# The expert stage's front with its router as the stationary operand and its rows normalised by ScalarE

## The reference, cut to what matters

```python
def _L1_ffn_ref(x, gate_w, gate_b, sw1, sb1, sw2, sb2, rw1, rb1, rw2, rb2):
    ...
    probs = jax.nn.softmax(x @ gate_w + gate_b, axis=-1)      # gate_w is 256 x 8
    topk_probs, topk_idx = jax.lax.top_k(probs, TOP_K)        # 2 of 8 experts
    cw = jnp.sum(jax.nn.one_hot(topk_idx, N_EXPERTS, dtype=x.dtype) * topk_probs[..., None], axis=2)
    hr = jnp.einsum('bsd,edf->ebsf', x, rw1) + rb1[:, None, None, :]
    out_e = jnp.einsum('ebsf,efd->ebsd', _swiglu(hr), rw2) + rb2[:, None, None, :]
    routed_out = jnp.einsum('ebsd,bse->bsd', out_e, cw)
    return shared_out + routed_out
...
x = x + 0.5 * _L0_ffn_ref(_layernorm(x, axis=-1), ...)
x = x + _L0_attn_ref(_layernorm(x, axis=-1), ...)
x = x + 0.5 * _L0_ffn_ref(_layernorm(x, axis=-1), ...)
x = x + 0.5 * _L1_ffn_ref(_layernorm(x, axis=-1), ...)
x = x + _L1_attn_ref(_layernorm(x, axis=-1), ...)
x = x + 0.5 * _L1_ffn_ref(_layernorm(x, axis=-1), ...)
```

## Time and profile before

| | us |
|---|---|
| three runs | 2554.85, 2563.77, 2571.64 |
| their median | 2563.77 |
| the profiled execution, its own time | 2565.47 |
| its span in the trace | 2563.6 |
| front of the first expert stage, first statistics to first use of the logits | 823.86 to 880.12 |
| the same of the second | 2088.27 to 2144.52 |

### The profile page before, as it was taken

One profiled execution on the slowest core, in us unless ns is written; L12 is line 12 of the kernel. 1 busy time (PEld: TensorE's weight loads), 2 busy tenths in 40 slices (PEclk: granted clock), 3 DMA queues, 4 the chain that ended last, 5 costly groups with the idle time before them and its releaser, 6 DMA issues. The chain is left out here.

```text
span 2563.6 us, 42162 instructions
## 1 busy us (share of the span) xinstructions
PE 2058.2 (80%) x11491; PEld 1356.1 (53%) x11492; DVE 1844.1 (72%) x3714; ACT 895.0 (35%) x1746; POOL 890.0 (35%) x889
## 2 busy tenths in 40 slices
PE   2599997689998658888776698998989865788885
PEld 1366666556665646677555233333333454567764
DVE  5698874498886776668976676776767377666696
ACT  1222224322222323333255255554555422233331
POOL 1344432144443656665245000000000035666641
PEclk9799997899999569999989699988989885899997
DMA  4000001100001512223336443334242024122234
GB/s 161 1 1 0 0 0 26 25 1 1 0 0 42 171 58 80 80 78 108 106 81 145 69 63 45 54 57 62 37 57 31 1 79 153 58 81 79 81 119 141
DMA packets 110245, 155.69 MB, mean 61 GB/s; under 512 B 20758, under 2 KB 77372, under 8 KB 109628
## 3 DMA queue, kind: packets, MB, share of 16 engines
q1 hardware_dynamic: 90416, 104.43, 18.1%
q0 software_dynamic: 17472, 48.80, 5.9%
q10 hardware_dynamic: 2252, 1.29, 0.2%
HBM read 107.00 MB, written 47.20 MB: 60 GB/s over the span
## 5 line engine op out<-in xcount | busy, mean ns | idle before, releaser
L1882 DVE TENSOR_REDUCE t_nm<-ps 128x1 f32<-128x512 f32 (+3 forms) x768 | 391.1, 552 | 152.9 <-PE ps L1972 75.4
L1948 ACT ACTIVATE t_E<-ps 128x1024 f32<-128x1024 f32 (+3 forms) x384 | 295.6, 808 | 280.1 <-PE ps L1998 225.9
L1377 PE MATMUL ps<-m_w,m_xT 128*128 (+1 forms) x1248 | 348.4, 415 | 0.0
L1377 PEld LDWEIGHTS ps<-m_w,m_xT 128*128 128x128 f32 x1248 | 223.5, 190 | 54.7 <-issue 4.4
L535 PE MATMUL ps<-wgT,f_xT 128*128 128x352 f32 x512 | 188.2, 517 | 37.0 <-DVE f_h L437 35.0
L496 POOL TENSOR_TENSOR f_h<-f_h,f_hmagic 128x704 f32<-128x704 f32 x64 | 108.0, 1688 | 298.4 <-DVE f_h L182 298.4
L1995 PE MATMUL ps<-t_Qs,t_Ks 98*128 98x512 bf16 (+3 forms) x768 | 208.0, 352 | 4.4 <-DMA t_Qs<-t_mT 3.4
L1867 POOL COPY t_Va<-t_V 128x128 f32 (+1 forms) x64 | 16.1, 295 | 542.2 <-DVE t_mp L1893 541.7
L1397 PE MATMUL ps<-m_w,m_hT 128*128 (+1 forms) x1248 | 202.0, 298 | 0.7 <-DVE m_hT L1476 0.7
L569 PE MATMUL ps<-wdT,f_hT 128*128 128x256 f32 (+1 forms) x768 | 191.1, 391 | 7.4 <-DVE X L472 5.4
L1967 PE MATMUL ps<-t_Ks,t_Qs 48*128 48x512 bf16 (+3 forms) x384 | 137.9, 359 | 70.4 <-DVE t_nm L1882 47.0
(11 more groups left out here) (285 smaller groups left out, 4078.0 us busy)
## 6 DMA issues: line engine op xcount, KB each, us to landing
m_yl<-m_picked_out SPq DMA_DIRECT2D x64, 256.0 KB, 2.8
m_raw<-in_L_ffn_rw SPq DMA_DIRECT2D x48, 256.0 KB, 3.3
t_parts<-t_qkv_part SPq DMA_DIRECT2D x64, 192.0 KB, 2.8
t_Qs<-t_parts SPq DMA_DIRECT2D x96, 128.0 KB, 4.2
t_Ks<-t_parts SPq DMA_DIRECT2D x96, 128.0 KB, 6.9
m_rows<-m_xn SPq DMA_DIRECT2D x16, 512.0 KB, 4.1
m_xg<-m_rows POOLq DMA_DIRECT2D x64, 128.0 KB, 3.1
X<-in_L_attn_x SPq DMA_DIRECT2D x4, 1024.0 KB, 14.2
```

What stands on the lines that cost most here:

```text
L1377: last = nc.tensor.matmul(ps[:, H1 + u, :], xT[:, u, kx, k, :], of_expert(w1, kw, e, k), start=n == 0, stop=n == 3 * DC - 1)
L1882: nc.vector.tensor_reduce(dst, ps[:, bank, 0:n], AX_X, ALU.max, negate=True).then_inc(emptied, 1)
L1948: nc.scalar.activation(E[:, s % NPB, :, 0:n], ps[:, bank:bank + 2, 0:n], ACT.Exp, scale=float(HD) ** -0.5).then_inc(e_ok, 1)
```

## The change

Three things change in the front, and their waits with them.

1. The logits: the router (16 or 8 columns) becomes the stationary operand and the 512 tokens of a group move, 4 matmuls in a group. The result has 16 rows by 512 tokens, in PSUM bank 6 or 7; ScalarE copies it to SBUF (`rows_from`), and TensorE turns it back with 4 transposes (`turn_logits`) into bank 4, as before.
2. `x_normalise` moves from VectorE to ScalarE, as scale times x plus a shift; the shift is made by a further VectorE and a further GpSimd instruction.
3. ScalarE's loop is written anew: `x_hi(g)`, `rows_from(g - 1)`, `x_normalise(g + 2)`, then the high halves of pieces 2g and 2g + 1, which stood at its head before.

```diff
--- before.py
+++ after.py
@@ -883,6 +883,7 @@
         w2 = ch.sb(name + "w2", [P, 2, SLOTS, FK, D], F32R, ctx=ctx)
         with ExitStack() as wctx:
             raw = ch.sb(name + "raw", [P, RAW, 512], ctx=wctx)
+            rowed = ch.sb(name + "rowed", [2 * EXPERTS, 2, GN], ctx=wctx)
         b1 = ch.sb(name + "b1", [P, SLOTS, 2 * FFE], ctx=ctx)
         b2 = ch.sb(name + "b2", [P, SLOTS, D], ctx=ctx)
         topw = ch.sb(name + "topw", [P, 2, TILES], ctx=ctx)
@@ -896,6 +897,8 @@
             router = ch.sb(name + "router", [P, DC, 2, EXPERTS], F32R, ctx=actx)
             mv = ch.sb(name + "mv", [P, 2, GT, 2], ctx=actx)
             veps = ch.sb(name + "veps", [P, 2, GT], ctx=actx)
+            nmean = ch.sb(name + "nmean", [P, 2, GT], ctx=actx)
+            shift = ch.sb(name + "shift", [P, 2, GT], ctx=actx)
             rstd = ch.sb(name + "rstd", [P, 2, GT], ctx=actx)
             small = ch.sb(name + "small", [P, 7, TILES], ctx=actx)
             taken = ch.sb(name + "taken", [P, TILES + 1, EXPERTS], BF16, ctx=actx)
@@ -918,7 +921,8 @@
                 sem, ("taken", "counted", "placed", "hot", "row_marked", "pick_marked", "tabled"))
             raw_in = [sem(f"raw_in{k}") for k in range(RAW)]
             xn_out = [sem(f"xn_out{k}") for k in range(2)]
-            XB_, LOGITS, COUNT, TABLE = (0, 1, 2, 3), 4, 5, 6
+            rows_ok, rows_out = sem("logit_rows"), sem("logit_rows_out")
+            LOGITS, COUNT, TABLE, ROWED = 4, 5, 6, (6, 7)
 
             def part(k):
 
@@ -954,6 +958,7 @@
                     for k in range(RAW + 2 * GROUPS, PIECES):
                         load_piece(k)
                     sp.wait_ge(w_split, PIECES)
+                    sp.wait_ge(logit_ok, GROUPS)
                     sp.dma_start(b1[:, 0:EXPERTS, :].rearrange("p e f -> p (e f)"),
                                  a['L1_ffn_rb1'].rearrange("e f -> (e f)").partition_broadcast(P)).then_inc(loaded_b, 16)
                     sp.dma_start(b1[:, SHARED, :], a['L1_ffn_sb1'][0].partition_broadcast(P)).then_inc(loaded_b, 16)
@@ -979,18 +984,10 @@
                         for j in range(GT):
                             nc.vector.bn_aggr(mv[:, b, j, :], ch.st6[:, j, :])
                         drain()
-                        ts(veps[:, b, :], mv[:, b, :, 1], EPS, None, ALU.add).then_inc(stats, 1)
-
-                    def x_normalise(g):
-                        b = g % 2
-                        dve.wait_ge(rstd_ok, g + 1)
                         if g >= 2:
-                            dve.wait_ge(x_turned, g - 1)
-                            dve.wait_ge(xn_out[b], 16 * (g // 2))
-                        for j in range(GT):
-                            last = ts(xn[:, b, j, :], ch.tile(g * GT + j), mv[:, b, j, 0:1], rstd[:, b, j:j + 1],
-                                      ALU.subtract, ALU.mult)
-                        last.then_inc(xn_ok, 1)
+                            dve.wait_ge(rstd_ok, g - 1)
+                        ts(veps[:, b, :], mv[:, b, :, 1], EPS, None, ALU.add)
+                        ts(nmean[:, b, :], mv[:, b, :, 0], -1.0, None, ALU.mult).then_inc(stats, 1)
 
                     def x_low(g):
                         dve.wait_ge(x_high, g + 1)
@@ -1017,10 +1014,7 @@
                     nc.vector.memset(taken[:, TILES, :], 0.0)
                     x_stats(0)
                     x_stats(1)
-                    x_normalise(0)
                     for g in range(GROUPS):
-                        if g + 1 < GROUPS:
-                            x_normalise(g + 1)
                         if g + 2 < GROUPS:
                             x_stats(g + 2)
                         x_low(g)
@@ -1140,8 +1134,12 @@
 
                     def x_rstd(g):
                         pool.wait_ge(stats, g + 1)
-                        nc.gpsimd.tensor_tensor(rstd[:, g % 2, :], veps[:, g % 2, :], ch.minus_half[:, :],
-                                                ALU.pow).then_inc(rstd_ok, 1)
+                        if g >= 2:
+                            pool.wait_ge(xn_ok, g - 1)
+                        nc.gpsimd.tensor_tensor(rstd[:, g % 2, :], veps[:, g % 2, :], ch.minus_half[:, :], ALU.pow)
+                        nc.gpsimd.drain()
+                        nc.gpsimd.tensor_tensor(shift[:, g % 2, :], nmean[:, g % 2, :], rstd[:, g % 2, :], ALU.mult
+                                                ).then_inc(rstd_ok, 1)
 
                     x_rstd(0)
                     x_rstd(1)
@@ -1178,15 +1176,24 @@
                         pe.wait_ge(x_stored, g + 1)
                         if g == 0:
                             pe.wait_ge(router_ok, 1)
+                        if g >= 2:
+                            pe.wait_ge(rows_out, g - 1)
+                        o = ps[0:2 * EXPERTS, ROWED[g % 2], :]
+                        for c in range(DC):
+                            nc.tensor.matmul(o, router[:, c, :, :].rearrange("p k e -> p (k e)"),
+                                             xT[:, g % 2, 0, c, :], start=c == 0, stop=False)
+                        for c in range(DC):
+                            last = nc.tensor.matmul(o[0:EXPERTS, :], router[:, c, 0, :],
+                                                    xT[:, g % 2, 1, c, :], start=False, stop=c == DC - 1)
+                        last.then_inc(rows_ok, 1)
+
+                    def turn_logits(g):
+                        pe.wait_ge(rows_out, g + 1)
                         for j in range(GT):
-                            o = ps[:, LOGITS, (g * GT + j) * 2 * EXPERTS:(g * GT + j + 1) * 2 * EXPERTS]
-                            for c in range(DC):
-                                nc.tensor.matmul(o, xT[:, g % 2, 0, c, j * P:(j + 1) * P],
-                                                 router[:, c, :, :].rearrange("p k e -> p (k e)"),
-                                                 start=c == 0, stop=False)
-                            for c in range(DC):
-                                last = nc.tensor.matmul(o[:, 0:EXPERTS], xT[:, g % 2, 1, c, j * P:(j + 1) * P],
-                                                        router[:, c, 0, :], start=False, stop=c == DC - 1)
+                            n = g * GT + j
+                            last = nc.tensor.transpose(ps[:, LOGITS, n * 2 * EXPERTS:(n + 1) * 2 * EXPERTS],
+                                                       rowed[:, g % 2, j * P:(j + 1) * P],
+                                                       ch.ident[0:2 * EXPERTS, 0:2 * EXPERTS])
                         last.then_inc(logit_ok, 1)
 
                     x_turn(0)
@@ -1194,6 +1201,9 @@
                         if g + 1 < GROUPS:
                             x_turn(g + 1)
                         logits(g)
+                        if g >= 1:
+                            turn_logits(g - 1)
+                    turn_logits(GROUPS - 1)
                     pe.wait_ge(taken_ok, 1)
                     every = (TILES + 1) * EXPERTS
                     nc.tensor.matmul(ps[:, COUNT, 0:every], ch.all_ones[:, :],
@@ -1226,15 +1236,40 @@
                     def x_hi(g):
                         act.wait_ge(x_turned, g + 1)
                         if g >= 2:
-                            act.wait_ge(logit_ok, g - 1)
+                            act.wait_ge(rows_ok, g - 1)
                         for c in range(DC):
                             last = nc.scalar.activation(xT[:, g % 2, 0, c, :], ps[:, 2 * (g % 2) + c, :], ACT.Copy)
                         last.then_inc(x_high, 1)
 
+                    def x_normalise(g):
+                        b = g % 2
+                        act.wait_ge(rstd_ok, g + 1)
+                        if g >= 2:
+                            act.wait_ge(x_turned, g - 1)
+                            act.wait_ge(xn_out[b], 16 * (g // 2))
+                        for j in range(GT):
+                            last = nc.scalar.activation(xn[:, b, j, :], ch.tile(g * GT + j), ACT.Identity,
+                                                        bias=shift[:, b, j:j + 1], scale=rstd[:, b, j:j + 1])
+                        last.then_inc(xn_ok, 1)
+
+                    def rows_from(g):
+                        act.wait_ge(rows_ok, g + 1)
+                        if g >= 2:
+                            act.wait_ge(logit_ok, g - 1)
+                        nc.scalar.activation(rowed[:, g % 2, :], ps[0:2 * EXPERTS, ROWED[g % 2], :], ACT.Copy
+                                             ).then_inc(rows_out, 1)
+
+                    x_normalise(0)
+                    x_normalise(1)
                     for g in range(GROUPS):
+                        x_hi(g)
+                        if g >= 1:
+                            rows_from(g - 1)
+                        if g + 2 < GROUPS:
+                            x_normalise(g + 2)
                         for k in range(2 * g, 2 * g + 2):
                             high_piece(k)
-                        x_hi(g)
+                    rows_from(GROUPS - 1)
```

## The result

The changed kernel takes 2591.89 us (median of 4 runs, 2584.92 to 2601.71), the kernel before 2560.64 (4 runs, 2554.85 to 2571.64): a ratio of **1.0125**, 95% interval 1.0095 to 1.0155. It is slower, by 31 us of medians, where 32 were forecast. The profiled execution took 2601.71 us, its span is 2599.9, 36.3 more than before.

What follows compares the result with a forecast made beforehand. The prediction took a ring over the rows' write to bound the fronts, lengthened by the change from 6.38 to 9.9 us a turn. 2 x 15.1 + 0.9 = 31.1 us on 2565.47 gave 2596.6, median forecast 2596, range 2581 to 2607.

Steps and rivals of the forecast that it cites:

- The ring of one turn: Changed loop: normalisation, high pieces, low pieces, rows' write and landing follow within one turn, 9.9 us against 6.38.
- The start: Front's beginning: first normalisation 3.64 us after the first statistics, at 827.5, and x_normalise(2) at 833.8.
- The tail: Front's end, behind x_normalise(7) at 883.3: VectorE reads the logits at 895.2 instead of 880.12, 15.1 us later.
- Sum: Whole kernel: 2 x 15.1 + 0.9 = 31.1 us longer, on 2565.47 giving 2596.6; median forecast 2596.
- The exponential: After the first front, behind ScalarE's pieces 16 to 22 and a table load: 898.9 against 898.0, 0.9 us lost.
- GpSimd's pieces were hidden: After the front: GpSimd's last 11 pieces, 14.25 us, end near 910, before its first marking at 921; costed at nothing.
- One ring sets the period: Fronts before: statistics, GpSimd's power and pieces, rows' write, landing and normalisation two turns later set the 6.38 us period.
- one link of that ring: From the end of GpSimd's second low piece to the next normalisation's start: 4.66 us, mean of nine.
- the rival of a faster kernel: In the fronts the engines bind, not the landing: turn 5.2 us, kernel 16 us faster, 2550; chance 0.04.
- the point of decision: Turn of 6.9 us down, needing 1.6 us instead of 4.66 between GpSimd's last piece and the normalisation.
- TensorE's time: Sign in the profile after: TensorE's busy time in the fronts down by half.
- The shorter landing: Rows' write lands sooner among less crowded DMAs, 3.1 us saving 10 us; page's 3.2 us included; 2586, chance 0.14.

Runs made afterwards that it cites:

- the two experiments above: The kernel before with each rows' write ahead of the loads, 2557.02 us, ratio 0.9990; the kernel before with no piece work in the groups' loop, 2581.95 us.
- the best kernel: The change with both orders, high pieces at the head of ScalarE's turn and rows' writes ahead of SP's loads: 2534.47 us, ratio 0.9893; again 2538.46, 0.9897.
- the kernel with turns of 6.51 us: The change with SP issuing the rows' write of group g + 1 ahead of the two loads of turn g: 2559.64 us, ratio 0.9987.
- the kernel with both orders and the power early: The change with high pieces first, rows' writes first and GpSimd's power and shift of group g + 3 ahead of the low pieces: 2550.00 us, ratio 0.9944.
- the kernel without pieces in the loop: The kernel before with all loads and splitting of expert weight pieces from the ninth on moved out of the groups' loop: 2581.95 us, one run.

## Why the prediction was right, point by point

- **The ring of one turn: right**, in place and size. Its terms in us, with what was said in brackets: the normalisation up to the first high piece 1.98 (1.95); first high to first low piece 0.69 (0.71); low pieces 2.50 (2.55); end of the low ones to the next normalisation 4.87 (4.66). That is a turn of 10.04, and 10.03 in the mean, against 9.9.
- **The start**: the third normalisation came 10.6 us after the first statistics, 9.97 said.
- **The tail missed a wait.** 14.56 us instead of 11.9. The logits were turned back at 899.14, 11.1 us after the last normalisation's start, so the part that was costed came out 0.8 us shorter than said. The missed term is VectorE's wait for the last rows' write, 3.5 us (2.8 in the second front), which stands in its code ahead of the first read. The sentence "VectorE reads the logits at 895.2" took the transposes as the last event. Most of it belongs to the same cause, SP held up by the moved high pieces: with these back at the head of the turn VectorE reads 1.4 us after the transposes' end in the first front (878.26 against 876.84) and right at their end in the second (2126.62 against 2126.58).
- **Sum**: the front came out 19.0 and 18.5 us longer, 15.1 said: 0.6 from the start, 0.6 from five turns, 2.7 from the tail. The median came out 4 us below the forecast all the same: the runs lost 31 us where the fronts of the profiled executions lost 37.6. Those two executions put 1.3 us of this outside the fronts; the rest lies within the interval of the ratio, 24 to 40 us. That the loss agrees with the forecast to about 1 us is therefore in part luck: the sum was 6.5 us too small, and the runs hid it.
- **The exponential** starts 2.93 us after the logits instead of 2.78, and not 0.9 later: the missed wait in the tail was time in which ScalarE went on with its pieces. The first marking follows the logits by 25.76 us, 25.22 before, so GpSimd's pieces were hidden as said.
- **Wrong: what bounds the fronts before.** "One ring sets the period" fell with the two experiments above. VectorE's stream, with its normalisations lengthened by GpSimd, is the bound. The forecast survived since it used only one link of that ring, whose length was read directly. For the rival of a faster kernel the prediction had good figures: ScalarE's own turn is 4.5 us in the best kernel (4.9 to 5.2 said), and the point of decision was put at a turn of 6.9 us, where the kernel with turns of 6.51 us stands at 0.9987. It lacked the reason for the gain: in that kernel no normalisation runs on VectorE, where GpSimd could hold it up.
- **Wrong in size: TensorE's time** in the fronts fell from 42.9 to 35.2 us, not by half. The first fronts as one stretch, before and after:

```profile
823.86:880.12 56.26, 42.86 (x192) 40.28 (x192) 46.00 (x121) 21.98 (x40) 33.81 (x31) 0.50 0.63 197
```

```profile
827.31:902.62 75.31, 35.22 (x128) 19.66 (x128) 25.84 (x98) 39.96 (x78) 33.27 (x37) 0.50 0.46 141
```

- **The shorter landing** (rival) did not come: 4.4 us median against 4.1. With it falls the estimate of 3.2 us for this write, which the prediction worked out from the Trainium skill, "DMA: Bandwidth & Descriptors", Anatomy of one DMA, whose line is for GpSimd's kind of DMA.

## What to carry to other kernels

When a step moves in one engine's stream, follow every queue behind it once round: the cost here was neither in the moved work nor in the added instructions but in the order of two queues, high pieces behind the normalisation on ScalarE and loads ahead of the write on SP. It vanished when either was turned round, and with both the kernel was 1% faster than before. Such rings nest, and the edit that opens the second can close a third, so each order is to be read anew. An engine that seems to wait briefly on a DMA may really be held by a neighbour: look at the longest of equal instructions before believing the releaser.

## What the runs showed of the hardware

- The rows' write of 512 KB took 4.4 us to land where the DMA engines were busy for 0.38 of the time, 4.1 where they were for 0.60, and 6.3 for the last of a front, which went out 2.5 us behind another write and among loads. Less traffic did not shorten it.
- GpSimd's pieces stretch one of VectorE's normalisations from 0.41 to 1.36 us, but not its statistics (1.40 for four) nor `x_low`, which reads PSUM (1.28), nor ScalarE's normalisation (2.08 for four). A product of two SBUF operands went from 0.42 to 1.24, and in one kernel to 8.66 and 10.16, as shown above. These rows are of the kernel with both orders and the power early, beside two pieces from 838.31 to 840.82:

```profile
838.15 1.29 DVE L1000 TENSOR_TENSOR m_xT<-ps,m_xT 128x512 fp32r<-128x512 f32 x2 [1.22 <-ACT m_xT L1247]
839.35 1.40 DVE L987 BATCH_NORM_STATS2 st<-X 128x6 f32<-128x256 f32 x4
```

- The granted clock did not follow how busy TensorE looks. Stretches of the kernel without pieces in the loop, then of the one with both orders, columns as above:

```profile
830.00:840.00 10.00, 10.00 (x49) 10.00 (x49) 9.62 (x36) 2.17 (x4) 2.38 (x3) 0.50 0.40 138
```

```profile
845.00:850.00 5.00, 3.60 (x16) 2.35 (x16) 3.79 (x14) 5.00 (x11) 3.72 (x5) 0.67 0.87 258
```

By its rows TensorE was busy throughout the first (the profile models the ends of matmuls), with the old logits' many small matmuls, and stayed at 0.50, the level of 1.2 GHz; in the second it was busy for 3.60 of 5 us with the logits as rows of 512, and was at the level of 2.4 GHz for a part of it. The fronts of the change itself, with the same instructions further apart, had 0.50. What grants the clock was not tried.
